# Experts' results in two halves of 64 groups, with the next attention's preparation between the second half's passes

## The reference

```python
grouped = x.reshape(b, s // g, g, d)                       # groups of 32 tokens: 128 groups in all
logits = jnp.einsum('bntd,des->bntes', grouped, Wc) + bc   # 32 x 4 = 128 experts
perm = (logits == jnp.max(logits, axis=-3, keepdims=True)) # each expert picks one token of each group
permuted = jnp.einsum('bntd,bntes->bnesd', grouped, perm)
inner = jax.nn.relu(jnp.einsum('bnesd,esdf->bnesf', permuted, W1) + b1)   # f = 32
result_permuted = jnp.einsum('bnesf,esdf->bnesd', inner, W2) + b2
result = jnp.einsum('bnesd,bntes->bntd', result_permuted, perm)
```

## Time and profile before

| what | us |
|---|---|
| median of 3 runs | 1509.73 (1505.41 to 1512.15) |
| the profiled execution | 1511.24 |
| its span, first to last instruction | 1509.5 |
| PE busy | 1334.6 (88%) |
| DVE busy | 905.7 (60%) |
| ACT busy | 589.4 (39%) |
| first results' matmul to first `scores` of the second attention | 620.5 to 786.65 |

### The profile page before, as it was taken

The page is one execution under the profiler, slowest core; times in us unless marked ns, Lnnn a source line. Parts: engine busy times, 40 slices in busy tenths (PEclk is TensorE's granted clock), DMA queues, the critical chain, the costliest instruction groups (busy, mean ns, idle before and its releaser), DMA issues.

```text
span 1509.5 us, 28422 instructions
## 1 busy us (share of the span) xinstructions
PE 1334.6 (88%) x10752; PEld 953.9 (63%) x10752; DVE 905.7 (60%) x1602; ACT 589.4 (39%) x1063; POOL 372.7 (25%) x324
## 2 busy tenths in 40 slices
PE   7877999999999878666777999999997789999997
PEld 5765677777777667411234676667665567777776
DVE  5875456665666446443544666556655477777772
ACT  4452444335442355333343334323432443333331
POOL 2541110111011100040013123113311554544441
PEclk9988999999999989987698999999999899999999
DMA  9996243134411585899969235524512211111101
GB/s 331 293 300 185 76 139 115 66 117 145 134 66 61 183 242 172 283 284 276 327 203 326 70 126 192 174 71 142 193 47 81 87 56 56 56 56 56 56 34 50
DMA packets 132726, 223.73 MB, mean 148 GB/s; under 512 B 25014, under 2 KB 46006, under 8 KB 129582
## 3 DMA queue, kind: packets, MB, share of 16 engines
q1 hardware_dynamic: 132654, 222.73, 45.2%
HBM read 131.47 MB, written 91.23 MB: 148 GB/s over the span
## 4 chain that ended last, share of the span: by engine, by line
PE 53%; issue 20%; DVE 9%; DMA 6%; ACT 5%; POOL 4%; SPq 2%; POOLq 0%; DVEq 0%; ACTq 0%
PE b L148 9%; PE b L150 8%; PE b L149 8%; PE b L1451 3%; PE b L1626 3%; PE b L1627 2%; PE b L1920 2%; PE b L1628 2%; PE b L1543 2%; DMA s_rp<-e_gt 2%; PE b L1552 2%; PE b L1950 2%; PE b L1423 2%; DVE f_mix L2138 2%; ACT e_gt L1830 1%
## 5 line engine op out<-in xcount | busy, mean ns | idle before, releaser
L1063 ACT ACTIVATE a_pr<-b 120x512 f32<-120x512 f32 x256 | 133.8, 602 | 104.2 <-PE b L1451 104.2
L1227 DVE TENSOR_REDUCE a_mx<-b 128x4 f32<-128x480 f32 x256 | 151.9, 650 | 3.8 <-PE b L1423 3.5
L1002 POOL TENSOR_TENSOR a_atl<-a_pvs,a_ath 128x512 fp32r<-128x512 f32 x64 | 81.3, 1294 | 222.3 <-ACT a_ath L1108 222.3
L963 POOL TENSOR_TENSOR a_rstd<-a_ve,a_mhalf 128x4 f32<-128x4 f32 x16 | 16.2, 1012 | 437.2 <-DVE a_ve L1176 437.2
L1626 PE MATMUL b<-a_woh,a_ath 128*128 128x512 f32 x256 | 106.2, 415 | 3.6 <-POOL a_atl L1002 3.6
L148 PE MATMUL b<-a_xth,a_wqh 128*128 128x512 f32 x256 | 104.5, 408 | 1.5 <-issue 1.5
L1627 PE MATMUL b<-a_wol,a_ath 128*128 128x512 f32 x256 | 102.8, 402 | 0.0
L1628 PE MATMUL b<-a_woh,a_atl 128*128 128x512 f32 x256 | 102.4, 400 | 0.0
L149 PE MATMUL b<-a_xtl,a_wqh 128*128 128x512 f32 x256 | 102.2, 399 | 0.0
L150 PE MATMUL b<-a_xth,a_wql 128*128 128x512 f32 x256 | 101.9, 398 | 0.0
L1350 DVE SCALAR_TENSOR_TENSOR a_x<-b,a_gate,a_x 128x512 f32 (+1 forms) x64 | 47.8, 747 | 86.4 <-PE b L1628 86.4
(11 more groups left out here) (229 smaller groups left out, 3238.1 us busy)
## 6 DMA issues: line engine op xcount, KB each, us to landing
a_rp<-s_rp SPq DMA_DIRECT2D x32, 1024.0 KB, 9.9
s_rp<-e_gt SPq DMA_DIRECT2D x32, 768.0 KB, 6.6
s_x<-a_x SPq DMA_DIRECT2D x16, 1024.0 KB, 4.3
kv_xb<-in_x SPq DMA_DIRECT2D x8, 1024.0 KB, 8.6
s_xn<-kv_xb SPq DMA_DIRECT2D x8, 1024.0 KB, 10.3
a_xn<-s_xn SPq DMA_DIRECT2D x8, 1024.0 KB, 7.8
a_x<-in_x SPq DMA_DIRECT2D x8, 1024.0 KB, 6.3
s_xn<-a_xn SPq DMA_DIRECT2D x8, 1024.0 KB, 5.0
```

The costliest lines, as they stand in the source:

```text
L1002: pool.tensor_tensor(atl[:, g], pvs[:, g], f(ath[:, g]), ALU.subtract).then_inc(a_lo, 1)
L1063: act.activation(pr[:, h % RING, :], bank[k][0:S2, :], ACT.Exp, scale=SCALE)\
L1227: dve.tensor_reduce(mx[:, t, :, r], bank[k][:, 0:HJ * S2].rearrange("p (a s) -> p a s", a=HJ), AX.X, ALU.max).then_inc(free[k], 1)
```

## The change

The 128 groups are done in two halves of 64, the first half with all 32 steps and then the second: 64 passes `p`. In a pass the four experts' matmuls take 64 columns (64 groups) and put two experts side by side on the 128 partitions of one bank, so two banks a pass, in turn 0, 1 and 2, 3 (`result_bank`). ScalarE evicts one and VectorE the other in the first half; in the second half ScalarE takes both of every odd pass. Two passes fill a slot of `out`, now with all 128 partitions, and SP stores it with one transfer of 1 MB, in pieces of 2 KB, once for each of 32 units `u`. `rp` is two DRAM tensors, one for each half, laid out expert by group by channel. The path of the first 32 groups is gone.

The second half's passes carry the preparation: merge at pass 39, turned x at 42, queries at 44, 46, 49 and 53, maxima at 47, 51, 55 and 57, `max_rows` at 59, the first `scores` after 63. SP loads x, perm, b2 and the query weight at unit 7, `rp` of sequence 0 at unit 18 behind a wait until all of the first half has landed (`half_written`), keys and bo at 20, v at 25, and perm and `rp` of sequence 1 at 28. x of sequence 1 still follows the last store. ScalarE's and VectorE's splits move to passes 22 to 26. GpSimd builds the tables only after pass 47 has read the last of `w2`'s second part, over whose room they now lie; several other tiles change rooms.

```diff
-LEAD_AT, LEADS, REST_SPLIT = 6, 4, 22
+             ("a1_pvs", (0, 4 * KB), "f_tmp"), ("e_b1", (0, 400), "f_mu f_gate f_stats f_mv f_mark f_ve f_rstd")]
+HALF = B // 2
 Engines = namedtuple("Engines", "sync gpsimd scalar vector tensor")
 LN_STEPS = 4
+MERGE_AT, NORM_AT, QUERIES_AT, MAXIMA_AT, ROWS_AT = 39, 42, (44, 46, 49, 53), (47, 51, 55, 57), 59
...
     def load_experts(sp, j, t):
-        src = io["rp"].rearrange("(j a t) e d -> e j t a d", a=GT, t=NT)
-        sp.dma_start(rp[:, t:t + 1], src[:, bass.ds(j, 1), t]).then_inc(rp_in[t], 16)
+        of = 0 if isinstance(j, int) and j < HALF else 1
+        src = io["rp"][of].rearrange("e (j a t) d -> e j t a d", a=GT, t=NT)
+        sp.dma_start(rp[:, t:t + 1], src[:, bass.ds(j - HALF * of, 1), t]).then_inc(rp_in[t], 16)
...
+    def spread_tables(pool):
+
+
+        steps = Steps(pool, fchain, CONST_STEPS[0][1] - 1)
+        picks = blank[:, 1, 0:C * S2].rearrange("p (c s) -> p c s", c=C)
+        steps.link(pool.memset(picks, 0.0))
+        for j in range(HJ):
+            steps.link(pool.affine_select(out=picks, in_=picks, compare_op=ALU.not_equal, fill=1.0, base=-DK * j,
+                                          pattern=[[-1, C], [0, S2]], channel_multiplier=1))
+        steps.link(pool.tensor_copy(mpick[:, :, :], picks))
+        steps.link(pool.memset(blank[:, :, :], 0.0))
+        spread = blank[:, :, :].rearrange("p g (q j i) -> p g q j i", q=C, j=HJ)
+        for q in range(C):
+            for d in range(2):
+                steps.link(pool.affine_select(out=spread[:, :, q], in_=spread[:, :, q], compare_op=ALU.not_equal,
+                                              fill=1.0, base=-8 * q - d, pattern=[[-2, C], [-DK, HJ], [0, DK]],
+                                              channel_multiplier=1))
+        steps.link(pool.tensor_copy(bc[:, :, :, :], blank[:, :, :].rearrange("p g (q n) -> p g q n", q=C)))
+        pool.drain().then_inc(const, 1)
+        steps.link(pool.memset(pick[:, :, :, :], 0.0))
+        for d in range(2):
+            steps.link(pool.affine_select(out=pick[:, :, :, :], in_=pick[:, :, :, :], compare_op=ALU.not_equal, fill=1.0,
+                                          base=-d, pattern=[[-2, C], [-8, C], [1, DK]], channel_multiplier=0))
+        pool.drain().then_inc(const, 1)
...
-    def load_behind(sp, k):
-
-
-        if k == 7:
+    def load_behind(sp, u):
+
+
+        if u == 6:
             sp.wait_ge(front.cleared, 1)
+        if u == 7:
             load_x(sp, 0)
             load_perm(sp, 0)
             sp.dma_start(b2[:, :], io["b2"]).then_inc(w_in[2], 16)
             load_gates(sp)
             sp.dma_start(bq[:, :], io["bq"]).then_inc(c_in, 16)
-        if k == 9:
             load_query_weight(sp)
-        if k == 15:
-            front.lead_written(sp)
-            sp.wait_ge(const, 3)
+        if u == 18:
+            front.half_written(sp)
             for t in range(NT):
                 load_experts(sp, 0, t)
-        if k == 19:
+        if u == 20:
+            sp.wait_ge(const, 2)
             load_keys(sp, 0)
-        if k == 21:
+            sp.dma_start(bo[:, :], io["bo"].partition_broadcast(P)).then_inc(bo_in, 16)
+        if u == 25:
             load_v(sp, 0)
-            sp.dma_start(bo[:, :], io["bo"].partition_broadcast(P)).then_inc(bo_in, 16)
+        if u == 28:
+            for k, uses in TW:
+                sp.wait_ge(full[k], uses.n(None, "merge", 1) + 1)
+            load_perm(sp, 1)
+            for t in range(NT):
+                load_experts(sp, 1, t)
...
             power(0)
+            front.half_read(pool)
+            spread_tables(pool)
...
-        def behind(pe, k):
-
-            if k == 19:
+        def behind(pe, p):
+
+            if p == 20:
                 pe.wait_ge(front.cleared, 1)
+            if p == MERGE_AT:
                 pe.wait_ge(e_lo, 1)
                 front.spare_banks(pe)
                 for t in range(NT):
                     merge_tile(None, 0, t)
-            if k == 21:
+            if p == NORM_AT:
                 first_norm(None, range(C))
-            if k == 23:
-                pe.wait_ge(w_lo[0], C)
-            if k in (23, 24):
-                queries(None, k - 23)
-            if k in (25, 27, 29, 30):
-                if k == 25:
-                    pe.wait_ge(const, 4)
+            if p in QUERIES_AT:
+                m = QUERIES_AT.index(p)
+                if m == 0:
+                    pe.wait_ge(w_lo[0], C)
+                queries(None, m)
+            if p in MAXIMA_AT:
+                r = MAXIMA_AT.index(p)
+                if r == 0:
                     pe.wait_ge(kbd_in, 16 * HJ)
                 for t in range(NT):
-                    max_tile(None, 0, {25: 0, 27: 1, 29: 2, 30: 3}[k], t)
-            if k in (26, 28):
-                queries(None, k // 2 - 11)
-            if k == EK - 1:
+                    max_tile(None, 0, r, t)
+            if p == ROWS_AT:
                 max_rows(None)
+            if p == 2 * EK - 1:
+                pe.wait_ge(const, 4)
                 front.banks(pe)
                 scores(None, 0, 0)
...
+    def result_on_act(p, q):
+
+        return q == 0 or (p >= EK and p % 2 == 1)
+
+    def result_bank(p, q):
+
+        b = 2 * (p % 2) + q
+        return b, uses(b, SETS * C) + p // 2
...
-        for k in range(EK):
-            for a in range(EJ):
-                sp.wait_ge(g_free[a], uses(a, SETS * C) + k + 1)
-            sp.dma_start(io["rp"][FIRST:, EJ * k:EJ * (k + 1), :], out[0:NG - FIRST, k % RO]).then_inc(out_st[k % RO], 16)
-            if lead_after(k):
-                store_lead(sp, k - LEAD_AT)
-            behind[0].load(sp, k)
-
-    def store_lead(sp, h):
-
-        for j in range(LEADS * h, LEADS * (h + 1)):
-            b, n = lead_bank(j)
-            sp.wait_ge(g_free[b], n + 1)
-        of = io["rp"][0:FIRST].rearrange("n (h k a) d -> h a n k d", a=EJ, k=LEADS)[h]
-        for a in range(EJ):
-            sp.dma_start(of[a], lead[h % 2][a * FIRST:(a + 1) * FIRST]).then_inc(lead_st[h % 2], 16)
-
-    def lead_written(sp):
-        for h in range(2):
-            sp.wait_ge(lead_st[h], 16 * EJ * (EK // LEADS // 2))
+        for u in range(EK):
+            for p in (2 * u, 2 * u + 1):
+                for q in range(2):
+                    b, n = result_bank(p, q)
+                    sp.wait_ge(g_free[b], n + 1)
+            steps = slice(4 * (u % (EK // 2)), 4 * (u % (EK // 2)) + 4)
+            sp.dma_start(io["rp"][2 * u // EK].rearrange("(s c) n d -> (c n) s d", c=2)[:, steps], out[:, u % RO])\
+              .then_inc(out_st[u % RO], 16)
+            behind[0].load(sp, u)
+
+    def half_written(sp):
+        for q in range(RO):
+            sp.wait_ge(out_st[q], 16 * len(range(q, EK // 2, RO)))
...
+        def results(p):
+            u = p // 2
+            if p % 2 == 0 and u >= RO:
+                act.wait_ge(out_st[u % RO], 16 * (u // RO))
+            for q in range(2):
+                if result_on_act(p, q):
+                    b, n = result_bank(p, q)
+                    act.wait_ge(g_full[b], n + 1)
+                    act.activation(out[:, u % RO, 2 * (p % 2) + q], gbank[b][:, :], ACT.Copy).then_inc(g_free[b], 1)
+            behind[0].act(act, p)
...
-        def results(k):
+        def results(p):
+            k, h = p % EK, p // EK
             if k % 4 == 0:
                 pe.wait_ge(relued, k // 4 + 1)
             if k % KS == 0:
                 pe.wait_ge(w2_in[k // KS], 16 * QUARTERS[k // KS])
+            for q in range(2):
+                b, n = result_bank(p, q)
+                pe.wait_ge(g_free[b], n)
             for a in range(EJ):
-                pe.wait_ge(g_free[a], uses(a, SETS * C) + k)
-            for a in range(EJ):
-                rows = slice(a * EF, (a + 1) * EF)
-                pe.matmul(gbank[a][0:NG - FIRST, :], inner[rows, k, FIRST:], w2[k // KS][rows, k % KS, :], start=True,
-                          stop=True).then_inc(g_full[a], 1)
-            for j in lead_after(k):
-                first_groups(j)
-            behind[0].pe(pe, k)
-
-        def first_groups(j):
-
-            if j == 0:
-                pe.wait_ge(relued, WG)
-            if j % KS == 0:
-                pe.wait_ge(w2_in[j // KS], 16 * QUARTERS[j // KS])
-            b, n = lead_bank(j)
-            pe.wait_ge(g_free[b], n)
-            for a in range(EJ):
-                rows = slice(a * EF, (a + 1) * EF)
-                ins = pe.matmul(gbank[b][a * FIRST:(a + 1) * FIRST, :], inner[rows, j, 0:FIRST],
-                                w2[j // KS][rows, j % KS, :], start=True, stop=True, skip_group_check=True)
-            ins.then_inc(g_full[b], 1)
+                rows, (q, c) = slice(a * EF, (a + 1) * EF), divmod(a, 2)
+                b, _ = result_bank(p, q)
+                ins = pe.matmul(gbank[b][c * NH:(c + 1) * NH, :], inner[rows, k, h * NH:(h + 1) * NH],
```

(45 more changed lines are left out.)

125 lines of the change are left out of this document (47 added, 78 removed).

## The result

The changed kernel takes 1487.98 us (median of 4 runs, 1482.63 to 1489.73), the kernel before beside it 1510.7 (1505.41 to 1512.15): ratio 0.985, 95% interval 0.9815 to 0.9885. It is faster by more than the 0.5% that can be told from nothing, and 5 us under the forecast of 1493. The profiled execution has a span of 1486.6 us against 1509.5.

The account below looks back on a forecast made before the run. The stage was taken as bound by stores first, then compute with gaps, then a hole waiting for loads. First `scores` at 770 instead of 786.65 us saves 16.6 us: 1509.7 - 16.6 = 1493 us, range 1484 to 1508.

Parts of the forecast that it names:

- A pass: In the results stage, four 32x64 matmuls were taken to last 1.04 us, bounds 0.96 and 2.08.
- Rival B: Row tiles that share a bank take turns, so a pass takes 2.08 us: 1538 us; chance 0.05.
- A store: Each 1 MB store of results from 128 partitions was taken at 2.72 us, bounds 2.63 and 3.4.
- rival A: The store queue is not kept full (stores at 3.4 us, or the clock falling between units): 1503 us; chance 0.20.
- The small loads: In the first half, x, perm, b2 and wq, all at unit 7, add 6.8 us between the stores.
- The added wait: At unit 18 SP waits for the first half; PE stands some 17 us, merges end at 714 us.
- Second half: From the merges' end to the first `scores`: 56 us, bounds 52 and 60.3, against 47.8 in the old kernel.
- x of sequence 1: Queued behind the last stores, x is there 15 us after the first `scores`.
- gain nil, -4 to +4: At turn 0's first merge a wait for x replaces the wait for rp: gain nil, between -4 and +4 us.
- Pool's tables: Table building of 17.4 us moves behind pass 47, covered by 31 us of work: cost nothing; uncovered 17 us.
- Rival C: rp's new layout, 128 KB from partition to partition, is read badly: 1527 us at 150 GB/s; chance 0.06.
- DMA work: The stage's stores fall from 117 to 87 us of DMA work, the old small stores taken at 0.94 each.

Follow-up runs that it names:

- The early x: The changed kernel with x of sequence 1 loaded ahead of stores 29 to 31 instead of behind them: 1482.38 us, ratio 0.979 to the kernel before.

## Why the prediction was right, and where its terms were off

The mechanism was right: stores that fill DMA cost less, and the preparation stands in the second half's passes. The stage was forecast to be 16.6 us shorter and was 16.7 shorter. That the two agree to 0.1 us is luck: by terms the merges were 0.8 us early, the second half 3.5 short and the wait for x 4.1 long, and these cancel. The other 5 us between 1493 and 1488 are the 4.6 ahead of the stage, which can be chance, and 1.5 behind, neither of them forecast. By steps, each from the stage's first matmul:

- **A pass** of four 32x64: 1.04 us taken, 0.94 measured. Rival B (2.08) is out: row tiles that write different partitions of one bank run side by side, also as two and two. The Trainium skill (TensorEngine Tiling (Array Packing), "Gotcha 1: PSUM Pressure") says that different row tiles can't access one bank at the same time. The trace disagrees: a pass of two such pairs takes 0.94 us and not twice as much.
- **A store** of 1 MB: 2.72 taken, 2.4 to 2.7 between units, DMA share 1.00 at 373 GB/s. Right within some 3% (1 MB at 373 GB/s is 2.81 us), and rival A is out: the queue stayed full although the clock was at 0.83 in that stretch. The engines' own unit was longer than the 2.1 I had: freed from the stores it is 2.34 (units begin at 686.81 and 689.15), with a 0.4 us wait for ScalarE's eviction, still under 2.72.
- **The small loads** at unit 7: 6.8 us taken; the gap 657.55 to 668.80 is 11.25, a store's 2.5 and 8.8 for them. With it SP reaches `rp` 73.8 us after the start; 71.5 forecast.
- **The added wait**: merges' end 93.5 us forecast, 92.7 measured. The stall of PE in it was mis-sized: 17 us forecast, 8.0 and 1.2 measured. I had let PE reach the merge long before; it reaches pass 39 only at 690, since its slots come free with the stores. The forecast of the end did not use that figure.
- **Second half**: 56 us taken with 52 as the lower bound, 52.5 measured. Passes of 0.94 make 2.4 of the difference, the waits inside the maxima (0.53 in place of 1.05, four times) 2.1; these make 4.5 of a difference of 3.5, so that some other term cost 1 more. VectorE evicts nothing in an odd pass, behind which the maxima stand; that this is the cause of the shorter waits was not tried.
- **x of sequence 1**: 15 us after `scores` taken, 19.1 measured. `perm` and `rp` were issued from 8.8 us ahead of `scores` and not 11, since the second half is shorter; `perm` and the 9 MB took 28 us and not 26. So the merge of turn 0 comes 19.1 us after `scores` where the old kernel had 14.9: the term "gain nil, -4 to +4" came out at its lower end, 4.2 us of loss, and cancelled what the second half had won. The early x shows that this is real time.
- **Pool's tables**: 728.69 to 746.1, within the cover of passes 48 to 63 (to 759). Nothing.
- **Rival C**: the old and the new layout tie, with `rp` at 9.8 us to landing against 9.9. Out.
- **DMA work**, 117 to 87 us: the 87 holds to 3 (32 x 2.81 = 90), the 117 does not. Over the stage the work fell by 15 us, by some 18 for equal bytes, so the old stores had cost 102 to 105: with 2.4 to 2.7 for each of 32 main ones, 16 to 28 are left for the small ones, 0.5 to 0.9 each and not 0.94. I had taken ten main stores for 644 to 713, where SP had issued fourteen by then and one had landed before; the last four small ones were issued only from 709.1 to 715.2. So the balance put work of main stores on the small ones. This didn't enter the sum, which was built forward from the new kernel's own costs. Had I forecast the gain as "work removed", 30 us, I would have been 13 over the stage's 16.7.

## What to carry to other kernels

In a stage that DMA fills, forecast the new schedule forward (landing by landing, with what each queue holds) and don't subtract removed work; then multiply share by length in one window over the stage before and after, which says in one number whether work went or gaps were filled, and compare the bytes of the two windows too. One transfer of all 128 partitions beat the same bytes in two of 64, and one of 96 cost as much as one of 128 when run singly and 0.9 of it when queued. When a load comes last behind a run of stores, look at its place in the queue first: here moving two lines gave 9 us.

## What the runs showed that I had not expected

- With one pair of banks the clock stayed at 0.50 to 0.52 from 650 to 737, where matmuls and evictions took turns (PE busy 65%), while the changed kernel's queued first half, 71% busy with waits for stores, had 0.83. A wait of 1 us in each pass cost 47 us in all; another us a pass came with it from the lower clock level. The shares of the two in the 47 us were not taken apart.
- 1 MB in two transfers of 64 partitions takes some 3.3 us of DMA work in place of 2.7 in the mean of the stage; run singly it takes 4.0. 32 us of the second half with two transfers:

```profile
729.00:761.00 32.00, 29.56 (x167) 14.04 (x165) 15.97 (x26) 13.98 (x25) 16.04 (x20) 1.00 0.90 235
```

  235 / 0.90 = 261 GB/s, against 228 / 0.63 = 362 with one.
- The same shape of work ahead of the stage began between 612.2 and 620.0 us from one execution to the next, so that a difference of a few us ahead of a change says nothing before it has been seen twice.
